# A four-layer graph kernel on one core: planned times moved by tables of constants before they set the order of engines and rings

## The reference, cut to what matters

```python
# layer 0: one head, additive scores        x = layernorm(x + elu(softmax(mask(leaky(s1 + s2))) @ (x @ W)))
# layer 1: 8 heads of width 32, dot product, then a feed-forward block, two inner layer norms
q, k, v = split(x @ w_qkv)
t = softmax(mask(q @ k.T / sqrt(32))) @ v
x1 = layernorm(x + t, ln1_g, ln1_b)
x1 = layernorm(x1 + relu(x1 @ w1 + b1) @ w2 + b2, ln2_g, ln2_b)
x = layernorm(x + x1)
# layer 2: 4 heads of width 64, additive scores, elu
# layer 3: one head                         e = leaky((x @ W1) @ (x @ W2).T);  x = layernorm(x + relu(softmax(mask(e)) @ (x @ W3)))
```

## Time and profile before

| | |
|---|---|
| median of three runs | 2973.89 us (2971.31 to 2974.82) |
| the profiled execution | 2974.13 us, its span 2972.3 us |
| busy in the span | PE 93%, ACT 89%, DVE 86%, POOL 79% |
| TensorE clock granted, mean | 0.981 |

### The profile page before, as it was taken

The page is one execution under the profiler, slowest core; times in us unless marked ns, Lnnn a source line. Parts: engine busy times, 40 slices in busy tenths (PEclk is TensorE's granted clock), DMA queues, the critical chain, the costliest instruction groups (busy, mean ns, idle before and its releaser), DMA issues. The chain is left out here.

```text
span 2972.3 us, 69732 instructions
## 1 busy us (share of the span) xinstructions
PE 2773.1 (93%) x22576; PEld 1510.7 (51%) x22576; DVE 2560.7 (86%) x8261; ACT 2659.7 (89%) x5079; POOL 2345.3 (79%) x2517
## 2 busy tenths in 40 slices
PE   5999999999999999999999999999999999999855
PEld 4444445555555555545555554555555455554433
DVE  6778889889989888998989999898998889889764
ACT  6668889899999999999999999999989999898974
POOL 5467779788878888887888888788887888887774
PEclk9999999999999999999999999999999999999978
DMA  7355567767767767776676767677777777676565
GB/s 172 71 99 107 104 118 133 140 118 143 136 133 127 139 131 135 128 140 129 129 143 129 139 131 135 123 137 133 136 129 136 130 134 140 125 129 118 108 114 100
DMA packets 1215804, 378.91 MB, mean 127 GB/s; under 512 B 1157712, under 2 KB 1194320, under 8 KB 1215440
## 3 DMA queue, kind: packets, MB, share of 16 engines
q1 hardware_dynamic: 1213616, 373.46, 67.6%
q10 hardware_dynamic: 1824, 0.99, 0.2%
HBM read 21.43 MB, written 16.78 MB: 13 GB/s over the span
## 5 line engine op out<-in xcount | busy, mean ns | idle before, releaser
L910 POOL TENSOR_TENSOR split_r<-prob_r,split_r 128x512 f16<-128x512 f32 x768 | 880.5, 1159 | 275.8 <-DVE split_r L1385 272.9
L1349 DVE CUSTOM_DVE_ANT_0 unused<-bank_ps,neg_mask 128x512 bf16<-128x512 f32 x1024 | 661.7, 684 | 121.0 <-PE bank_ps L1561 120.3
L1627 PE MATMUL bank_ps<-val_r,trans_r 128*128 128x64 f16 (+1 forms) x9216 | 631.7, 222 | 72.9 <-DMA trans_r<-split_r 72.2
L1627 PEld LDWEIGHTS bank_ps<-val_r,trans_r 128*128 128x128 f16 x9216 | 526.9, 99 | 252.5 <-DMA trans_r<-split_r 74.8
L1154 ACT ACTIVATE prob_r<-bank_ps 128x512 f32<-128x512 f32 x1024 | 571.6, 607 | 48.7 <-PE bank_ps L1579 43.5
L1133 ACT ACTIVATE prob_r<-masked_r,low_r 128x512 f32<-128x512 f32 x768 | 535.8, 722 | 41.0 <-DVE low_r L1334 35.6
L1385 DVE TENSOR_SCALAR_CACHE_REDUCE split_r<-prob_r 128x512 f16<-128x512 f32 x768 | 510.9, 677 | 49.6 <-ACT prob_r L1133 25.7
L1587 PE MATMUL bank_ps<-prob_r,value_ones 128*33 128x512 f32 (+1 forms) x2048 | 546.1, 611 | 0.1
L1334 DVE CUSTOM_DVE_ANT_0 masked_r<-bank_ps,neg_mask 128x512 f32<-128x512 f32 x768 | 507.9, 683 | 31.0 <-ACT bank_ps L1122 22.9
L1578 PE MATMUL bank_ps<-stack 98*128 98x512 f16 x1024 | 393.3, 384 | 0.4 <-DVE low L1349 0.2
L1579 PE MATMUL bank_ps<-neg_mask_t,identb 128*128 128x512 bf16 x1024 | 389.6, 381 | 0.0
(11 more groups left out here) (148 smaller groups left out, 4532.7 us busy)
## 6 DMA issues: line engine op xcount, KB each, us to landing
stack<-qk SPq DMA_DIRECT2D x384, 128.0 KB, 2.4
xcur<-in_x_dram SPq DMA_DIRECT2D x32, 512.0 KB, 4.0
out_dram<-z SPq DMA_DIRECT2D x32, 512.0 KB, 3.1
trans_r<-split_r SPq DMA_TRANSPOSE x768, 3.3
xt_r<-split_r SPq DMA_TRANSPOSE x320, 3.3
stack<-low_rows SPq DMA_DIRECT2D x128, 4.0 KB
qk<-in_adj_dram SPq DMA_DIRECT2D x1, 1024.0 KB, 7.9
z<-in_L_gnn_W_dram SPq DMA_DIRECT2D x4, 256.0 KB, 12.3
```

The lines of the kernel that those rows point to most:

```text
L910: nc.gpsimd.tensor_tensor(split_r[:, j, 1, :], prob_r[:, i, :], split_r[:, j, 0, :], ALU.subtract).then_inc(lo_done.sem, 1)
L1349: nc.vector.tensor_tensor_reduce(out=unused[:, nth % 2, :], in0=bank_ps[entry("bank", "sq", g, t, b, h)][:], in1=neg_mask[:, b, :], scale= ...
L1627: ins = nc.tensor.matmul(bank[:, at:at + width], trans_r[:, i, pp, jb, :], val(g, layer)[:, vp, jb, cols], start=(n == 0), stop=(n == len( ...
```

## The change

`schedule` stays as it is, but its result now is the order and the planned start of every task. A new function `settle` moves each start by a constant of the task's kind (`NUDGE`), a constant of its place in the graph's list of 492 (`OFFSET`), and one of its graph (`DRIFT`, empty here). All tasks are sorted by the moved start, and from the sorted list come the queues of the engines and, in one pass with one clock for all rings, the buffers and their previous owners. A buffer goes to the entry whose last closing task ends earliest by the moved times. No instruction is added, removed or resized. `PW_RUN` is 0 and does nothing. The code below it stands 81 lines further down, so line 1627 before is line 1708 after.

```diff
+    NUDGE = {"add_0": -1.4, "add_1": 1.5, "add_3": -0.1, "ap_0": 0.5, "ap_2": 1.6, "ap_3": 0.7, "ap_ffn": -0.2, "ap_out": -0.3,
...
+    OFFSET = {0: 0.1, 1: 0.4, 2: 1, 3: -0.2, 4: 0.9, 8: -0.4, 9: 0.5, 11: 0.1, 12: 0.6, 14: -0.3, 16: 0.7, 17: 0.2, 18: -0.8,
...
+    DRIFT = {}
+    PW_RUN = 0
...
+                start[best] = now
...
-        return order, place, before, max(ends.values())
-
-    ORDER, PLACE, BEFORE, LENGTH = schedule()
+        return order, start, max(ends.values())
+
+    def settle(order, start):
...
+        moved, closers = {}, {}
+        for key, (_, us, _, _, closes, lands, (_, nth)) in tasks.items():
+            begin, ahead = start[key], 0.0
...
+            moved[key] = begin + NUDGE.get(kind_of(key), 0) + OFFSET.get(nth - first[key[1]], 0) + DRIFT.get(key[1], 0) - ahead
+            for entry in closes:
+                closers.setdefault(entry, []).append(key)
+        place, before = {}, {}
+        entries = {name: [[-1e18, None, n] for n in range(size)] for name, size in POOLS.items()}
+        in_turn = sorted(tasks, key=lambda key: (moved[key], tasks[key][6][1]))
+        for key in in_turn:
+            for name, opener in tasks[key][3]:
+                if (name, opener) in place:
+                    continue
+                entry = min(entries[name], key=lambda e: (e[0], e[2]))
+                place[name, opener], before[name, opener] = entry[2], entry[1]
+                entry[0] = max(moved[k] + tasks[k][1] + tasks[k][5] for k in closers[name, opener])
+                entry[1] = opener
+        return {engine: [key for key in in_turn if tasks[key][0] == engine] for engine in order}, place, before
+
+    PLANNED, START, LENGTH = schedule()
+    ORDER, PLACE, BEFORE = settle(PLANNED, START)
```

More of the change, by code:

```diff
@@ L122, in graph_layers_kernel @@
     SHIFT = {}
+    NUDGE = {"add_0": -1.4, "add_1": 1.5, "add_3": -0.1, "ap_0": 0.5, "ap_2": 1.6, "ap_3": 0.7, "ap_ffn": -0.2, "ap_out": -0.3,
[4 rows of a table added]
+             "job_hi_k": -3.3, "job_hi_s2": -1.4, "job_hi_v": 0.2, "job_k": -1, "job_lo_c0": 0.2, "job_lo_f2": 0.2, "job_lo_g":
[9 rows of a table added]
+    OFFSET = {0: 0.1, 1: 0.4, 2: 1, 3: -0.2, 4: 0.9, 8: -0.4, 9: 0.5, 11: 0.1, 12: 0.6, 14: -0.3, 16: 0.7, 17: 0.2, 18: -0.8,
[32 rows of a table added]
+    DRIFT = {}
+    PW_RUN = 0
     STEP = {"add_0": 1.22, "add_1": 1.23, "add_3": 1.23, "ap_0": 0.97, "ap_1": 0.99, "ap_2": 0.98, "ap_3": 0.98, "ap_ffn": 0.98,
@@ L369, in schedule @@
         open_entries = {}
+        start = {}
         now, left = 0.0, len(tasks)
@@ L433, in schedule, with kind_of @@
                 now = events[0]
-        return order, place, before, max(ends.values())
-    ORDER, PLACE, BEFORE, LENGTH = schedule()
+        return order, start, max(ends.values())
+    def settle(order, start):
+        def kind_of(key):
+            return f"{key[0]}_{key[2]}" if key[0] in BY_STAGE else key[0]
+        moved, closers = {}, {}
+        for key, (_, us, _, _, closes, lands, (_, nth)) in tasks.items():
+            begin, ahead = start[key], 0.0
+            if key[0] == "pw" and PW_RUN > 1:
+                run = [(*key[:3], kb) for kb in range(key[3] // PW_RUN * PW_RUN, key[3] // PW_RUN * PW_RUN + PW_RUN)]
+                begin = max(start[k] for k in run)
+                ahead = 1e-4 * (tasks[run[-1]][6][1] - nth)
+            moved[key] = begin + NUDGE.get(kind_of(key), 0) + OFFSET.get(nth - first[key[1]], 0) + DRIFT.get(key[1], 0) - ahead
[15 more added lines that the diff above has]
+    ORDER, PLACE, BEFORE = settle(PLANNED, START)
     print("planned", LENGTH, {e: round(sum(tasks[k][1] for k in ORDER[e])) for e in ORDER})
```

## The result

The kernel after took 2947.43 us, median of 4 runs (2943.33 to 2952.21), beside 2974.36 us for the kernel before on the same chip (2971.31 to 2976.77). The ratio is 0.992, with a 95% interval of 0.990 to 0.993: 27 us or 0.9% faster, against 23 us forecast. One execution of a variant (`e7_after_pw_pairs`) took 15336.83 us and is left out of its median. Most of the predicted steps are seen. One part of the gain is not in the prediction at all, though: PE itself got quicker, with the same instructions. The experiments are there to find how.

What follows compares the result with a forecast made beforehand. The prediction took PE as the bound, with 82.3 us idle in the middle. Its terms, -6.5 - 6.6 - 12 - 3 + 5 = -23.1 us, gave 2951 us from 2974; own range 2940 to 2965, 8 of 10 runs 2925 to 2982.

Steps and rivals of the forecast that it cites:

- Spreads: PE's wait at layer 2's fourth spread for DVE's `nd`, 7.8 us; a `pv` moved between wins 6.5 us.
- Value projection: PE's wait at the value projection for DVE's `job_lo`; another bank, freed by `mk`, wins all 6.6 us.
- "absorbed" rival: PE's waits are won at these places and come back at the next one: 2974 us, chance 0.12.
- Last `u` and stack: Earlier last `u` starts the `stack` earlier; dense products wait less for turned rows: 12 of 26.2 us won.
- Transposed tiles: PE's waits of 23.3 us at the `pv` for transposed tiles; 3 us won.
- New waits: Moves take cover away elsewhere and banks change hands: 5 us lost, bounds nothing and 17.2 us.
- The ends: Last 173 us, chains of single graphs: no move shortens a chain, 0 us, with 8 us to each side.
- No order can win more than a part of 82.3 us in the middle: 82.3 us is PE's idle time from 200 to 2800 us; order without change of work acts only through waits.
- near 60 us in the middle: Sign of being right: PE's idle time from 200 to 2800 us falls to near 60 us.
- One sign that it named as "wrong": Lines appear in which PE waits for DVE in banks it did not wait for before.
- the slower one through DVE: An advanced reciprocal heads DVE's queue, waiting for an unfinished `pv`, delaying `hi_v`, `nd` and `mk`: 2985 us, chance 0.16.
- The larger gain: Transposes as a whole come earlier, half of PE's 82.3 us goes and 8 us at the end: 2925 us, chance 0.17.

Runs made afterwards that it cites:

- e7_after_pw_pairs: Kernel after, with each pair of heads' four `pw` put in two pairs, each at the later one's place: 3047.28 us, ratio 1.026.
- e8: Kernel after, with the constants of `nr`, `nd`, `bc` and the spreads of layer 2 taken back: 2945.35 us, ratio 0.992.
- e9: Kernel after, with the constants of the last two rounds of `u` and `pw` of layer 1 taken back: 2950.02 us, ratio 0.994.
- e10: Kernel after, with the constants of layer 3's `mk` and layer 0's `job_lo` taken back: 2944.43 us, ratio 0.990.
- e4: Kernel after, with the constants only on tasks of PE, the other engines' set to zero: 3055.9 us, ratio 1.028.
- e5: Kernel after, with the constants on all tasks but those of PE, whose queue is that of before: 3004.65 us, ratio 1.011.
- mb_neighbours: Small kernel without the computation: matmuls alone, two kinds alternating one by one, then four by four; 48 changes fewer saved 5.99 us with `pw`-shaped tasks.

## Why the prediction was right, and where it was not

The forecast of 2951 us was 3.6 us above the time, inside the range. Its steps, one by one, with the predicted terms cut to the 20 graphs, which are 1758 of the 2600 us that the prediction had as the middle (x 0.68):

- **Spreads, -6.5 us.** The mechanism is right: the wait was removed, and came back with the edit. It reads as 4.6 us in the 20 graphs (4.4 by the prediction), a difference as small as that between two executions, and about 1 us in the time, which is not to be told from nothing.
- **Value projection, -6.6 us.** The wait went and came back too, and the time is the same with and without it. Its 4.0 us in the 20 graphs (4.5 by the prediction) are no cost either: this kernel was 4 to 7 us ahead of after at graph 8, and at graph 28 it stands level with it. The wait for turned rows took up what the projection lost. So this term is worth nothing, where 6.6 us were taken: it is the "absorbed" rival in small. That `mk` would be in time was nearly right; 2.9 us of waits for it are left, where none were counted.
- **Last `u` and stack, -12 us.** The wait fell from 26.2 to 14.8 us, near the half that was taken. Taken back: 9.9 us in the 20 graphs (8.1 by the prediction), 6 us in the time, both with a wait for ACT in them that isn't the term's. This was "the largest term", and of the three it is; as a size it was at least twice too large.
- **Transposed tiles, -3 us.** The wait fell by 7.1 to 9.6 us, from 23.3 to 16.2 and 13.7 in the two profiles. No run took this alone back.
- **New waits, +5 us.** Lines of 4.4, 3.4 and 2.9 us are there in the 2574 us: about 11 us where 5 were taken, inside the bound of 17.2 us.
- **The ends, 0.** They took 6 us more, and nearly all of it lies behind graph 28: from there to the end the kernel after loses 4.4 and 6.6 us of its lead, `e8` 1.8, `e9` 2.7 and `e10` 4.9. That is within the 8 us that were left open. Which task of the last graphs does it, no run isolates; it stays open.
- **"No order can win more than a part of 82.3 us in the middle, and a change of order without any change of work can only win or lose through waits."** This step failed. PE's pace itself depends on the order: by the paces 10.7 us of the 33 in the 20 graphs, and by busy time in `e10` 14.1 us of 29.9, came out of time that the page calls busy. The row for it was in the earlier trace rows, where the two matmuls of a `u` start 0.22 us apart and a `pw` needs 1.01 us; no `pw` on end with another was laid beside it.

So the sum was near in part by luck, for errors that cancel. Its total of waits was about right in the steady part (15.7 us of idle time there, 22 us by the table, 16 by the prediction's sum x 0.68), but some 5 us were lost in the last graphs, and the pace, which it left out, filled the place: about 18 us in 32 graphs by the price of a change. Nor do its terms stand for themselves: taken back one by one, the three of 6.5, 6.6 and 12 us cost 1, 0 and 6 us, 7 of the 27 us. Idle time "near 60 us in the middle" is 67 us in the two traces that can be read for it. One sign that it named as "wrong" is there, new lines in which PE waits for DVE, but PE's waits for DVE as a whole did not grow (25.9 us before, 23.7 and 22.4 after).

Of the rivals, the slower one through DVE has its beginning (18.3 us in 31 waits at the reciprocal, from 11.0 in 17), but PE's waits for DVE did not grow by it. What it costs when the moves don't go together is seen in `e4` and `e5`, there mostly through ACT: 84 and 33 us, by the 2972.09 us of the kernel before measured beside them. The "absorbed" rival holds for one term, the value projection, and not for the whole. The larger gain was not there: the transposes' waits in the last 172 us are 43.1 us as before.

## What to carry to other kernels

Count how often a TensorE queue changes between tasks on parts of the array and tasks on the whole of it, before saying that an order can win only idle time; but a longer run of one kind must fit the banks and the engine that empties them, or the waits eat more than the changes save. Test a term of such a sum by taking back a chain of tasks on all its engines, and look at where along the run the difference arises: a wait that is won may be handed on to the next one, and a lead may shrink in the last graphs. Compare the counts of matmuls and weight loads before comparing idle times.

## What the runs showed of the hardware

- A change between a part of the array (64 columns or 32 rows) and the whole, or between two kinds of part, costs 0.11 to 0.13 us at the granted clock of 1.00, in float32 as in 16 bits (`mb_neighbours`); 128x128 in float32 beside 128x128 in 16 bits costs nothing. All of it is shown as busy.
- At such a change the weight load starts with its matmul; without one it starts 0.22 us ahead (92.28 and 190.84 us in the rows of `mb_neighbours`).
- Two matmuls on the two halves of 64 columns ran side by side: 32 of such pairs with 32 `whole`, four by four, took 22.54 us, where two on the same 64 columns took 29.42 us. That is 0.215 us less each, the step from one matmul of 512 columns to the next:

```profile
274.60:297.14 22.54, 22.54 (x130) 8.54 (x129) 0.00 (x0) 1.00 0.00 1
```
